# Feed-forward products by seven block products each: one level of Strassen's scheme, weight sums on GpSimd

## What is computed

```python
def _rfs(xw, ab, AB, gs):
    dot_products = jnp.einsum('...d,rd->...r', xw, ab[:, None] * gs)
    correction = (0.5 * jnp.sum(xw * xw, axis=-1))[..., None] * (ab * ab)
    return 1.0 / math.sqrt(NUM_RFS) * AB * jnp.exp(dot_products - correction)

weights = _rfs(input_weights, ab, AB, proj_matrix)   # 1024 x 1024
feats = _rfs(x, ab, AB, proj_matrix)                 # tokens x 1024
attn = jnp.einsum('bsr,or->bso', feats, weights)
x = _layernorm(x + attn)

gate = jnp.einsum('bsd,hd->bsh', x, wg)              # 1024 -> 3072
up = jnp.einsum('bsd,hd->bsh', x, wu)                # 1024 -> 3072
h = jax.nn.silu(gate) * up
x = _layernorm(x + jnp.einsum('bsh,dh->bsd', h, wd)) # 3072 -> 1024
```

## Time and profile before

| | |
|---|---|
| median of 3 runs | 700.57 us (700.29 to 701.27) |
| the profiled execution | 700.95 us |
| its span, first to last instruction (slowest core) | 699.4 us |
| spans of the 8 cores | 695.3 to 699.4 us |
| busy: TensorE, VectorE, ScalarE, GpSimd | 94%, 29%, 27%, 5% |
| mean granted TensorE clock | 0.98 of full |

### The profile page before, as it was taken

The page is one execution under the profiler, slowest core; times in us unless marked ns, Lnnn a source line. Parts: engine busy times, 40 slices in busy tenths (PEclk is TensorE's granted clock), DMA queues, the critical chain, the costliest instruction groups (busy, mean ns, idle before and its releaser), DMA issues.

```text
span 699.4 us, 8152 instructions; the slowest of 8 cores (695.3 to 699.4 us)
## 1 busy us (share of the span) xinstructions
PE 657.8 (94%) x3084; PEld 298.4 (43%) x3084; DVE 203.6 (29%) x351; ACT 191.9 (27%) x314; POOL 37.6 (5%) x63
## 2 busy tenths in 40 slices
PE   3869949999989999999999999999999999999995
PEld 1324414455544444444444444444444444444442
DVE  0445472556531212121112122221212121112212
ACT  2356733466652121111112011212121111111101
POOL 9000220000000000000000000000000000000000
PEclk9989989999999999999999999999999999999998
DMA  8998030143109312311220110113111300001011
GB/s 110 160 171 280 2 120 1 36 145 121 61 1 410 132 61 69 112 61 60 84 97 31 60 61 31 60 61 119 62 61 67 114 1 0 1 31 61 30 61 60
DMA packets 12710, 57.15 MB, mean 82 GB/s; under 512 B 1536, under 2 KB 1536, under 8 KB 9216
## 3 DMA queue, kind: packets, MB, share of 16 engines
q0 software_dynamic: 7920, 39.85, 20.1%
q1 hardware_dynamic: 4752, 16.78, 6.4%
HBM read 40.90 MB, written 8.39 MB: 70 GB/s over the span
## 4 chain that ended last, share of the span: by engine, by line
PE 78%; DVE 7%; ACT 7%; issue 4%; DMA 2%; POOL 1%; DVEq 0%; ACTq 0%; POOLq 0%
PE P L447 46%; PE P L480 24%; PE P L291 3%; DVE z L403 3%; PE P L259 3%; DMA proj<-projT 2%; ACT junk L373 2%; DVE acc L203 2%; DVE arg L249 1%; ACT fe L251 1%; DVE sqw L218 1%; ACT lnst L374 1%; PE P L231 1%; ACT sqw L212 1%; PE P L322 0%
## 5 line engine op out<-in xcount | busy, mean ns | idle before, releaser
L447 PE MATMUL P<-x1t,ring 128*128 128x512 bf16 x1536 | 332.3, 380 | 1.5 <-ACT x1t L429 1.5
L447 PEld LDWEIGHTS P<-x1t,ring 128*128 128x128 bf16 x1536 | 150.0, 98 | 182.4 <-issue 1.9
L480 PE MATMUL P<-wdb,hact 128*128 128x512 bf16 x768 | 166.1, 380 | 0.0
L471 DVE SCALAR_TENSOR_TENSOR hact<-P,hact 128x512 bf16<-128x512 f32 x96 | 66.3, 692 | 259.7 <-PE P L447 256.6
L469 ACT ACTIVATE hact<-P 128x512 bf16<-128x512 f32 x96 | 57.1, 597 | 253.5 <-PE P L447 253.4
L480 PEld LDWEIGHTS P<-wdb,hact 128*128 128x128 bf16 x768 | 75.1, 98 | 90.7
L373 ACT ACTIVATE junk<-z 128x1024 bf16<-128x1024 f32 x32 | 33.8, 1057 | 168.0 <-DVE z L496 145.8
L259 PE MATMUL P<-xf,proj 128*128 128x512 bf16 x256 | 62.2, 404 | 14.6 <-DMA proj<-projT 14.4
L384 PE MATMUL P<-wt,fe 128*128 128x512 bf16 x256 | 57.5, 380 | 0.0
L496 DVE SCALAR_TENSOR_TENSOR z<-P,x1k 128x1024 f32<-128x1024 f32 x16 | 19.6, 1225 | 104.5 <-PE P L480 104.5
L259 PEld LDWEIGHTS P<-xf,proj 128*128 128x128 bf16 x256 | 25.9, 103 | 51.4 <-issue 25.9
(11 more groups left out here) (41 smaller groups left out, 159.6 us busy)
## 6 DMA issues: line engine op xcount, KB each, us to landing
ring<-wgu POOLq DMA_DIRECT2D x24, 1024.0 KB, 5.0
xtok_sb<-xtok SPq DMA_DIRECT2D x16, 512.0 KB, 3.2
out<-z SPq DMA_DIRECT2D x16, 512.0 KB, 2.6
wdb<-wd POOLq DMA_DIRECT2D x3, 2048.0 KB, 14.6
xf<-xfm POOLq DMA_DIRECT2D x16, 256.0 KB, 25.7
proj<-projT POOLq DMA_DIRECT2D x8, 256.0 KB, 17.2
iw<-iwT POOLq DMA_DIRECT2D x4, 512.0 KB, 40.1
xisc_sb<-xisc SPq DMA_DIRECT2D x1, 4.0 KB, 1.7
```

Source lines behind the costliest of these rows:

```text
L447: fn = lambda e: e.matmul(bank(b), lhsT, rhs, start=(dk == 0), stop=(dk == DK - 1))
L471: t_h[pss, hc] = freed[b0 + 2 + j] = p.mark("vector", lambda e, j=j, h=h: e.scalar_tensor_tensor(h, bank(b0 + 2 + j), 1.0 / 16129.0, h, OP ...
L480: fn = lambda e: e.matmul(bank(b), lhsT, rhs, start=(hc == 0), stop=(hc == HC - 1))
```

## The change

Each of the three feed-forward products is cut into 2 x 2 blocks, on the side of the weights and on the side of the tokens, and made from seven block products instead of eight (one level of Strassen's scheme). Seven left operands are four blocks and three to five sums or differences of blocks; so are the right ones. Blocks are numbered 0 to 3, sums 4 to 6, and sums 3 and 2 replace blocks 3 and 2 in place; `sums` makes all five of them.

- *Weights of gate and up.* A ring slot now has room for seven blocks; there are two slots. GpSimd loads a slot and makes its five sums for gate and for up (`ring_sums`: ten additions of 128x512 in bf16).
- *Weights of down.* GpSimd loads them in six parts early in the kernel, makes five sums of 128x1024 of each (`stage_load`, `stage_sums`) and stores all seven blocks in HBM (`t_hbm`); part 0 stands between the loads of `xf`, parts 1 to 3 behind the loads of `iw`, parts 4 and 5 behind the weight units. In the down stage SyncE loads one block of 1.5 MB for each product, into three buffers in turn.
- *Tokens.* All 2048 tokens go in one pass, as two pairs of tiles. `x_sums` makes five sums of 128x2048 for each pair, on GpSimd and VectorE, once within and once behind the attention stage. In the down stage VectorE makes the sums of `hact` (`s_sum`).
- *x1k* keeps four blocks only; each is stored in HBM (`x1_hbm`) from SyncE's queue when it is ready, and loaded again for the last addition.
- *Gate and up* is 24 units of 56 matmuls (`gate_up`), evicted by 14 operations on VectorE, 6 on ScalarE and 2 on GpSimd for each. *Down* is 14 products of 48 matmuls, whose parts are added up in `zd` by VectorE and GpSimd; the norm of a token block comes in two halves.

The core of the diff:

```diff
+    def sums(view, toks, plan):
+        out = {0: toks, 1: toks}
+        todo = ((6, 0, 2, OP.add), (4, 0, 1, OP.add), (3, 3, 0, OP.subtract), (5, 3, 1, OP.add), (2, 2, 1, OP.subtract))
+        todo = [todo[i] for i in (0, 1, 3, 2, 4)]
+        for (o, i, j, op), eng in zip(todo, plan):
+            behind = {3: out.get(5), 2: out.get(6)}.get(o, ())
+            out[o] = (p.mark(eng, lambda e, o=o, i=i, j=j, op=op: e.tensor_tensor(
+                view(o), view(i), view(j), op), *toks, *behind),)
+        return out
+    def stage_load(c):
+        s = c % 2
+        ld_stage[c] = load(f"ld_stage{s}", ring[:, s * SLOT:s * SLOT + 4096],
+                           wd_h[:, c * 4096:(c + 1) * 4096], st_stage.get(c - 2))
+    def stage_sums(c):
+        s = c % 2
+        done = sums(lambda i: slot_block(s, i), (ld_stage[c],), ["gpsimd"] * 5)
+        st_stage[c] = p.dma(
+            "gpsimd", f"st_stage{s}", t_hbm[:, :, c * 1024:(c + 1) * 1024],
+            ring[:, s * SLOT:(s + 1) * SLOT].rearrange("p (k n) -> p k n", k=7), *[done[o][0] for o in (6, 4, 5, 3, 2)])
+    for k in range(4):
+        load_x(1, k)
+    stage_load(0)
+    for t in (2, 3):
         for k in range(4):
             load_x(t, k)
+    stage_sums(0)
     for k in range(4):
         ld_iw[k] = load(f"ld_iw{k}", iw[:, k * 2048:(k + 1) * 2048], iwT_h[:, k * 2048:(k + 1) * 2048])
+    for c in (1, 2, 3):
+        stage_load(c)
+        stage_sums(c)
...
+    def ring_sums(n, w):
+        w_sum[n, w] = sums(lambda i: slot_block(n % 2, i, w * 512, w * 512 + 512), (ld_ring[n],), ["gpsimd"] * 5)
...
     for n in range(4):
         u = w_unit(n, mid=norm_w_mm(t_accw) if n == 0 else None)
         w_evict(n, *u)
+    for c in (4, 5):
+        stage_load(c)
+        stage_sums(c)
+    for n in range(2):
+        load_ring(n, st_stage[4 + n])
+        for w in range(2):
+            ring_sums(n, w)
...
         ln1[i] = p.mark("vector", lambda e: e.tensor_scalar(
-            x1k[:, o:o + 1024], z, negm, rstd, OP.add, OP.mult), t_r, t_mm1)
+            x1k[:, o:o + 1024], z, negm, rstd, OP.add, OP.mult), t_r, t_mm1, turned.get(i - 4), st_x1.get(i - 4))
+        st_x1[i] = p.dma("sync", f"st_x1{i % 4}", x1_hbm[i * 128:(i + 1) * 128, :], x1k[:, o:o + 1024], ln1[i])
...
     for i in range(NM):
         attn(i)
         if i >= 2:
-            turn(i - 2)
+            turn(i - 2, 6 + i % 2)
+        if i == 11:
+            x_sums(0, ["gpsimd", "gpsimd", "vector", "vector", "gpsimd"])
...
+    def gate_up(u, n, pr, w):
...
+        t4 = product(4, n, pr, w, bB, True, True, freed[bB])
+        c4 = p.mark("scalar", lambda e: e.activation(eb, bank(bB), AF.Copy, scale=sc), t4, eb_free.get(par))
+        t5 = product(5, n, pr, w, bC, True, True, freed[bC])
+        e1 = p.mark("vector", lambda e: e.scalar_tensor_tensor(eb, bank(bC), -sc, eb, OP.mult, OP.add), t5, c4)
+        t1 = product(1, n, pr, w, bA, True, True, freed[bA])
+        e2 = p.mark("vector", lambda e: e.scalar_tensor_tensor(eb, bank(bA), sc, eb, OP.mult, OP.add), t1, e1)
+        t6 = product(6, n, pr, w, bZ, True, True, freed[bZ])
...
+        t2 = product(2, n, pr, w, bB, False, True, c4)
+        t3 = product(3, n, pr, w, bC, False, True, e1)
+        t7 = product(7, n, pr, w, bA, True, True, e2)
...
+        wb_free[par] = p.mark("gpsimd", lambda e: e.tensor_tensor(h[1, 1], wb, h[1, 1], OP.mult), w3, sg)
+        eb_free[par] = p.mark("gpsimd", lambda e: e.tensor_tensor(h[0, 0], eb, h[0, 0], OP.mult), e3, sg)
...
+    units = [(0, 0), (1, 0), (0, 1), (1, 1)] + [(n, pr) for n in range(2, HP) for pr in range(2)]
+    for u, (n, pr) in enumerate(units):
+        gate_up(u, n, pr, 0)
+        if u == 0:
+            turn(NM - 2, 6)
+        gate_up(u, n, pr, 1)
+        if u == 0:
+            turn(NM - 1, 3)
+            x_sums(1, ["gpsimd", "vector", "vector", "vector", "gpsimd"])
+        if pr == 1 and n + 2 < HP:
+            load_ring(n + 2, unit_pe[u])
+            for w in range(2):
+                ring_sums(n + 2, w)
...
+    for i in range(14):
+        pr, k = i // 7, SEQ[i % 7]
+        down(i)
```

More of the change, by code:

```diff
@@ L429, in turn, with x_block, x_sums @@
         t_x1t[i] = freed[b] = p.mark("scalar", lambda e: e.activation(dst, src, AF.Copy), tok, t_mm1)
+    x_op = {}
+    def x_block(pr, i):
+        if i < 4:
+            row, col = ((0, 0), (1, 1), (0, 1), (1, 0))[i]
+            o = (2 * pr + col) * 4096 + row * 2048
+            return x1t[:, o:o + 2048]
+        o = (pr * 3 + i - 4) * 2048
+        return xsum[:, o:o + 2048]
+    def x_sums(pr, plan):
+        toks = tuple(t_x1t[i] for i in range(8 * pr, 8 * pr + 8))
+        x_op[pr] = sums(lambda i: x_block(pr, i), toks + (t_mm1,), plan)
     for i in range(NM):
@@ L504, in build_nc @@
[L504 to L517 removed]
+    eb_free, wb_free = {}, {}
@@ new lines, in build_nc, with hslot, product @@
+    unit_pe = {}
+    def hslot(s, half, tile):
+        o = s * 4096 + half * 2048 + tile * 512
+        return hact[:, o:o + 512]
+    def product(k, n, pr, w, b, start, stop, *tokens):
+        i, j = A_BLOCK[k], B_BLOCK[k]
+        for dk in range(4):
+            lhsT = slot_block(n % 2, i, w * 512 + dk * 128, w * 512 + (dk + 1) * 128)
+            rhs = x_block(pr, j)[:, dk * 512:(dk + 1) * 512]
+            fn = lambda e, dk=dk, lhsT=lhsT, rhs=rhs: e.matmul(
+                bank(b), lhsT, rhs, start=(start and dk == 0), stop=(stop and dk == 3),
+                skip_group_check=not start)
+            if dk == 3:
+                return p.mark("tensor", fn)
+            p.run("tensor", fn, *w_sum[n, w][i], *x_op[pr][j], *tokens)
@@ new lines, in build_nc, with load_t, xr @@
+    SEQ = (4, 5, 1, 3, 7, 2, 6)
+    last = len(units) - 1
+    ld_t, t_pe = {}, {}
+    def load_t(i):
+        b = i % 3
+        first = {0: (unit_pe[last - 2],), 1: (unit_pe[last - 1],),
+                 2: (unit_pe[last], *t_h[last])}.get(i, ())
+        ld_t[i] = p.dma("sync", f"ld_t{b}", tbuf[b][:, :], t_hbm[:, B_BLOCK[SEQ[i % 7]], :],
+                        *first, t_pe.get(i - 3), *[st_stage[c] for c in range(6)])
+    ld_xr = {}
+    xr_done = {}
+    def xr(row, m):
+        o = ((1 - row) * 4096 if row else 0) + m * 1024
+        o = row * 4096 + m * 1024
+        return xres[:, o:o + 1024]
@@ new lines, in load_xr @@
+    def load_xr(pr, row, m):
+        i = 8 * pr + 4 * row + m
+        behind = (ln1[NM - 1],) if row else (unit_pe[last], *t_h[last])
+        ld_xr[pr, row, m] = p.dma("sync", f"ld_xr{row}{m}", xr(row, m), x1_hbm[i * 128:(i + 1) * 128, :],
+                                  st_x1[i], *(behind if pr == 0 else (xr_done[0, m],)))
+    for m in range(4):
+        load_xr(0, 1, m)
+    load_t(0)
+    load_t(1)
+    for m in range(4):
+        load_xr(0, 0, m)
+    load_t(2)
+    s_op = {}
+    s_used = {}
@@ new lines, in down @@
+    def down(i):
+        pr, k = i // 7, SEQ[i % 7]
+        o = A_BLOCK[k]
+        ready = s_op[pr, o] if o > 1 else None
+        view = s_view(pr, o)
+        t_b = tbuf[i % 3]
+        for m in range(4):
+            b = (4 * i + m) % 8
+            for s in range(HP):
+                lhsT = view[:, s, m * 128:(m + 1) * 128]
+                rhs = t_b[:, s * 512:(s + 1) * 512]
+                fn = lambda e, lhsT=lhsT, rhs=rhs, s=s, b=b: e.matmul(
+                    bank(b), lhsT, rhs, start=(s == 0), stop=(s == HP - 1))
+                if s == HP - 1:
+                    tok = p.mark("tensor", fn)
+                elif s == 0:
+                    p.run("tensor", fn, ld_t[i], ready, *h_done[pr], freed[b])
+                else:
+                    p.run("tensor", fn)
+            down_evict(pr, k, m, b, tok)
+        t_pe[i] = tok
+        if o in (6, 4, 5):
+            s_used[{6: 0, 4: 1, 5: 0}[o]] = tok
+        if i + 3 < 14:
+            load_t(i + 3)
@@ L519, in build_nc @@
+    s_sum(0, 6)
+    for i in range(14):
+        pr, k = i // 7, SEQ[i % 7]
+        down(i)
+        if k == 4:
+            s_sum(pr, 4)
+        elif k == 5:
+            s_sum(pr, 2)
+        elif k == 1:
+            s_sum(pr, 5)
+        elif k == 3:
+            s_sum(pr, 3)
+        elif k == 2 and pr == 0:
+            s_sum(1, 6)
+            for m in range(4):
+                load_xr(1, 1, m)
+                load_xr(1, 0, m)
+    p.wait("sync", *st_out.values())
     with nc.Block() as block:
```

271 lines of the change are left out of this document (171 added, 100 removed).

## The result

The changed kernel takes **789.8 us** (median of 4 runs, 788.43 to 794.08) against 700.82 for the kernel before on the same chip: a ratio of 1.128, 95% interval 1.123 to 1.133. I had forecast 754 us and 722 to 786: slower, as said, but 36 us further than the forecast and 4 us outside the range.

The account below looks back on a forecast made before the run. Feed-forward time was taken as a count of TensorE matmuls, the front as waits for sums. On 700.95 us: -62.2 + 44 + 54 + 2 + 6 + 8 + 1 = +52.8, forecast 754 us, 8-in-10 range 722 to 786.

Parts of the forecast that it names:

- Removed matmuls: Gate, up and down products: 288 fewer matmuls at 0.216 us each, -62.2 us.
- The front: Before attention: four rounds of weight sums delay GpSimd's norm additions, so TensorE resumes later, +44 us (29 to 62).
- The store in SyncE's queue: Attention: each x1k store holds back the next token load, 3.6 us, 15 times, +54 us (45 to 68).
- GpSimd beside VectorE and slow clock in attention: Attention: GpSimd and VectorE hold each other up, +6 us (2 to 12); TensorE partly at 1.2 GHz, +2 (0 to 8).
- the lock on x1k: Rival, attention: GpSimd holds x1k up like L218, all 6 us, 757 us in all; chance 0.05.
- Start of gate and up: First gate and up units: VectorE's x sums and a shorter first ring round cost +8 us (3 to 12).
- Down: Down product: loads, sums and additions all covered, nothing on the path but the end.
- two products' time to land: Down product: each 1.5 MB load has two products of 10.4 us to land and takes 4 us plus 2.5.
- The tail: End of down: VectorE spends 3.3 us per token block against TensorE's 2.6, last chain 1.0 us shorter, +1 us.
- GpSimd pacing gate and up at 785 us: Rival, gate and up: from 1.33 us per 128x512 operation GpSimd's ring round passes 24.2 us; 785 us; chance 0.14.
- tokens in time: Rival, attention: the store doesn't hold back the token load, the 54 us go, 700 us; chance 0.08.

Follow-up runs that it names:

- e10_rebuilt: Changed kernel with token loads ahead, loads issued inside sums, norm additions behind three rounds, x sums on VectorE, z22 additions spread: 675.2 us, 0.964 of the kernel before.
- e2_norm_on_vector: Changed kernel with the three additions of the weights' squares moved from GpSimd to VectorE: 759.1 us, 1.082 of the kernel before.
- e5_gpsimd_beside: Kernel before with 26 idle 128x1024 float32 additions on GpSimd beside its attention stage: 717.0 us, 1.022 of the kernel before.
- e9_z22_later: Changed kernel with two of GpSimd's three z22 additions of each pair moved from product 2's evictions to product 7's: 790.2 us, 1.127 of the kernel before.
- e1_tokens_ahead: Changed kernel with token loads issued up to three blocks ahead of the x1 stores in SyncE's queue: 727.7 us, 1.037 of the kernel before.
- e3_both: Changed kernel with token loads ahead of the x1 stores and the norm's three additions on VectorE: about 711 us, 1.013 of the kernel before.
- e6_other_banks: Changed kernel with the banks of gate and up exchanged between the two weights: 794.0 us, 1.132 of the kernel before.
- e7_down_order: Changed kernel with down loads issued ahead of output stores and x1k loads, two z22 additions one product earlier: 794.0 us, 1.132 of the kernel before.

## Why the prediction was right in direction and short in size

Over the span, 52.8 us were forecast and 93.1 measured. The paths were the right ones, and the terms of the sum on them too small: the front by 7.6 us, attention by 19.6 (the token waits by 12.8, GpSimd beside VectorE and the clock together by 2, the hand-over to gate and up, 4.0, had no term, and 1 is unexplained), the start of gate and up together with down by 10.8 (down's wait had been put at nothing), the tail by 2.3.

- **Removed matmuls, -62.2: right.** 96 matmuls of the down product run from 740.07 to 760.79 us, 0.216 each as in the earlier trace rows. In `e10_rebuilt` gate, up and down take 450.9 us against 500.9 before; 9.6 of that are waits (all those above but the first), and without them it is 441.3 where the count of matmuls asks for 438.7.
- **The front, 44 predicted, 51.6 measured: right mechanism, landings mis-sized.** The first sums began at 37.5 (I had 35) and ended at 51.3 (50). Load 1 landed at 78.2, not 72: behind `iw` in the same queue it needed 23.4 us from issue. Then rounds of 22.7 us in place of 21.6. One bf16 addition took 2.12 us, less than my 2.4, but a landing 10.7 in the median, not 8.5. GpSimd's norm additions were over at 145.1, not 137.5: 7.6 us. (In the kernel before, the last load was issued by 18.9 us and not at 17, as the earlier trace rows have it; nothing hangs on that.) `e2_norm_on_vector` shows that these additions carry 45 of the 51.6 us. The other 7, hidden behind them in the changed kernel, lie earlier: VectorE's additions for the tokens' norm, now with GpSimd's sums beside them, took 1.72 us in the mean (L259) and 1.56 (L281), in the kernel before 1.23 and 0.69 (L203 and L225 in the earlier trace rows). A load behind the 1.8 MB store took 5.6 us longer to land than one of the same size in the ring (medians 10.7 against 5.1 of `ring<-wgu`); I had allowed 3.5, less than the 5 us between two loads of 2 MB.
- **The store in SyncE's queue, 54 predicted, 66.8 measured: right mechanism, too small.** The waits above have 62.4 us in 14 waits for tokens (62.0 with the stores alone). The fifteenth, 4.4 us, stands there as one for TensorE, but block 9's tokens and its last matmul came at the same time, and the chain that ended last goes through the tokens (the wait in VectorE's timeline, then the chain):

```profile
268.01 1.22 DVE L466 SCALAR_TENSOR_TENSOR z<-P,xtok_sb 128x1024 f32<-128x1024 f32 x1 [4.40 <-PE P L447]
...
264.06 3.86 DMA xtok_sb<-xtok
268.01 1.24 DVE z L466 x2
```

  An undisturbed block waits 3.95 us (I had 3.6: landings took 3.3 to 3.6, not 3.0 to 3.2). And I costed 15 undisturbed blocks; the second waited 9.5 us, its load landing 8.9 us after issue, beside a 1.8 MB store and the ring's first megabyte.
- **GpSimd beside VectorE and slow clock in attention, 6 + 2 predicted, 10 and nothing measured: wrong in x1k and in the one-column operations.** From the first z to the last, the stage is 138.0 us against 60.4, +77.6. VectorE's timeline splits it: 66.8 waiting for tokens; 3.9 because x1k took 1.07 in the mean; 3.5 because the one-column L433 took 0.39 and not 0.16; 2.4 of its own x sums. That is 76.6; 1.0 us stays unexplained. TensorE's attention matmuls took 70.8 us at a mean clock of 0.81 in place of 57.5, but behind the first block no z waited for them alone. I gave the lock on x1k the chance 0.05 as a rival and half its price in the sum, and the one-column operations nothing: `e5_gpsimd_beside` says that x1k is held up and, of the one-column operations, the one with two inputs. The x sums themselves cost less than I had put: VectorE's two fell where GpSimd was idle. These two groups of the attention stage after answer to x1k's in the earlier trace rows:

```profile
L473 DVE TENSOR_SCALAR x1k<-z,lnst 128x1024 bf16<-128x1024 f32 x15 | 16.1, 1074 | 18.9 <-ACT lnst L439 18.9
...
L433 DVE SCALAR_TENSOR_TENSOR lnst<-lnst 128x1 f32<-128x1 f32 x15 | 5.9, 392 | 1.6
```

- **A step that was missing, 4.0 us.** Before, TensorE began gate and up 2.6 us ahead of the last z (191.01 and 193.62), as it needed neither its bank nor its block. After, it begins 1.4 us behind it, in the bank that this z reads. The stage's end is then VectorE's chain, not TensorE's; I had asked which wait ends last inside the stage and not who hands over to the next one.
- **Start of gate and up, 8 predicted: right in its part, and the clock missed.** The waits are 1.4 (x1t) and 6.3 us (VectorE's three x sums, 8.3 us beside GpSimd's); the old wait for x1t of 1.5 us goes. But behind the 12.9 us hole TensorE began at 1.2 GHz, and its first 16 matmuls took 6.1 us in place of 3.5; behind the 6.3 us hole the clock was at 0.50 again, and 16 took 5.8:

```profile
328.00:329.00 1.00, 1.00 (x4) 0.44 (x3) 0.65 (x1) 0.00 (x0) 0.00 (x0) 0.50 0.82 252
330.00:331.00 1.00, 1.00 (x7) 0.41 (x6) 0.69 (x2) 0.00 (x0) 0.00 (x0) 1.00 1.12 262
```

  (windows of one us behind the first hole, columns as in the earlier trace rows: the clock is the 0.50, then 1.00). I had priced neither.
- **Down, 0 predicted, 8.1 measured: the step that failed is "two products' time to land".** A 1.5 MB load took 5.8 to 17.8 us to land; one was 5.5 late, and the product behind it took 13.1 us in place of 10.5, at 1.2 GHz to begin with. It was issued at 712.85 us, though the last product that reads its buffer was over at about 701. I had compared a mean landing with the time of two products and not asked what else SyncE's queue holds between the two pairs: eight loads of x1k that wait for GpSimd's last additions, and four stores behind them (SyncE's timeline, 696 to 713 us); but the runs with another order did not make it better.

```profile
696.37 13.04 SPq L80 DMA_DIRECT2D xres<-x_hbm  x8
709.51 3.25 SPq L80 DMA_DIRECT2D out<-zd  x4
712.85 38.14 SPq L80 DMA_DIRECT2D tbuf<-t_hbm  x5
```

- **The tail, 1 predicted, 3.3 measured: the wrong engine's chain.** I had counted VectorE's work per token block, 3.3 us. The blocks follow each other at 4.28 us, and the chain that ended last runs there through GpSimd's three z22 additions a block, not through VectorE:

```profile
779.28 1.17 POOL zd L717
780.58 2.83 POOL zd L717 x2
783.55 1.16 POOL zd L717
```

  VectorE's last eviction waits 1.1 us for them. The two also hold each other up: beside them VectorE's one-column L699, with two inputs, takes 0.8 to 1.2 us where it takes 0.2 alone, and the first of GpSimd's three up to 1.7 where it takes 1.3. In `e9_z22_later`, with two of the three additions gone from here, VectorE starts later, and the tail is 10.2 us in place of 10.8.
- **The rivals.** GpSimd pacing gate and up at 785 us comes nearest to the number, and did not happen: its operations of 128x512 took 1.16 us (L589 and, in the mean, the ring's sums) and 1.33 (L590), 1.18 in the mean of a round's fourteen, below my 1.27 and the 1.33 at which it decides, and it idled 115.7 us behind VectorE. That its number comes so near is chance: the same total came out of other places. This row tells the two apart:

```profile
L589 POOL TENSOR_TENSOR hact<-wbuf,hact 128x512 bf16<-128x512 f32 x24 | 27.8, 1157 | 115.7 <-DVE wbuf L586 115.7
```

  The estimate from the Trainium skill (GPSIMD Engine Reference, section "Performance versus the Vector engine") is 1.29 us for float32; this trace has 4.04 us for 2048 columns in bf16 beside the page's 4.497. The rival "tokens in time" had the right place and a fair price for it: `e1_tokens_ahead` gives 62 us back.
- **The range.** Its upper end came from one rival alone on top of the middle values. The terms that failed (landings, x1k and L433 beside GpSimd, the missed hand-over, the clock behind the holes, down, the tail) all erred to the dear side at once, in stages where nothing covers them, and I had summed no such case.

## What to carry to other kernels

A scheme that saves matmuls only pays if its sums and stores stay out of the queues by which the rest is fed: here 62 us saved cost 155, some 110 of it for one store's place in SyncE's queue and one set of additions' place in GpSimd's; with these places changed, loads issued inside the sums and the x sums off GpSimd, the same scheme wins 3.6%. When an in-order queue issues a transfer and then waits for it, issue it one piece of work earlier, and cost a landing by what stands ahead of it and beside it in all queues, not by its size. After removing two delays, expect a third that they hid (30 us in `e3_both`), and cost any GpSimd sum of two tensors as time taken from VectorE's operations beside it that read two SBUF inputs, the one-column ones included, and from wide ones like x1k. When a bank or a queue is exchanged to remove a wait, ask by which other queue the same wait can come back (`e6_other_banks`, `e7_down_order`).
